# Cross attention: one product with V moved ahead inside its step, and one exponential ahead of an eviction

## What is computed

```
q_c = _ln(x) @ W_qc + b_qc
kv_c = _ln(context) @ W_kvc + b_kvc
k_c, v_c = jnp.split(kv_c, 2, axis=-1)
...
c_attn_w = jax.nn.softmax(jnp.einsum('bhqd,bhsd->bhqs', q_c, k_c) * scale, axis=-1)
c_attn_out = jnp.einsum('bhqs,bhsd->bhqd', c_attn_w, v_c)
```

## Time and profile before

| | us |
|---|---|
| median of 3 runs | 2712.4 |
| lowest, highest | 2710.79, 2716.66 |
| the profiled execution | 2714.79 |
| its span | 2712.8 |

### The profile page before, as it was taken

One profiled execution on the slowest core, in us unless ns is written; L12 is line 12 of the kernel. 1 busy time (PEld: TensorE's weight loads), 2 busy tenths in 40 slices (PEclk: granted clock), 3 DMA queues, 4 the chain that ended last, 5 costly groups with the idle time before them and its releaser, 6 DMA issues. The chain is left out here.

```text
span 2712.8 us, 49884 instructions
## 1 busy us (share of the span) xinstructions
PE 2616.2 (96%) x18548; PEld 2150.8 (79%) x18548; DVE 1708.4 (63%) x3413; ACT 1126.3 (42%) x2187; POOL 1303.5 (48%) x1447
## 2 busy tenths in 40 slices
PE   8899999999789999999999999999799999999997
PEld 6688888888578888888888888887478888888886
DVE  6677777776727777777777777776654444444431
ACT  4354444444434555555555555554432212212210
POOL 1445445454415777777777777767611221220211
PEclk9999999999889999999999999999799999999999
DMA  7454545545243444444444444334231111111110
GB/s 221 127 131 118 130 124 137 129 117 153 85 131 98 113 113 112 109 112 113 118 113 111 111 120 117 107 89 124 83 113 36 43 47 36 43 47 36 43 43 24
DMA packets 190609, 269.86 MB, mean 99 GB/s; under 512 B 32769, under 2 KB 110593, under 8 KB 190353
## 3 DMA queue, kind: packets, MB, share of 16 engines
q1 hardware_dynamic: 187296, 259.33, 35.4%
q0 software_dynamic: 3072, 7.34, 0.8%
HBM read 111.11 MB, written 36.77 MB: 55 GB/s over the span
## 5 line engine op out<-in xcount | busy, mean ns | idle before, releaser
L1639 ACT ACTIVATE cross_prT<-cross_tr_ps 125x448 f32<-125x448 f32 x768 | 407.4, 544 | 285.0 <-PE cross_tr_ps L1389 275.9
L1517 DVE TENSOR_REDUCE cross_parts<-cross_sc_ps 112x1 f32<-112x500 f32 x512 | 336.9, 664 | 213.3 <-PE cross_sc_ps L1375 212.0
L1690 POOL TENSOR_TENSOR cross_part<-cross_prT 125x448 f32<-125x448 f32 x252 | 291.7, 1157 | 212.8 <-PE cross_or_ps L1409 113.7
L1013 POOL TENSOR_TENSOR self_psum<-self_prT 112x224 f32<-112x224 f32 x256 | 180.9, 707 | 331.0 <-ACT self_prT L903 321.0
L1389 PE MATMUL cross_tr_ps<-cross_qst,cross_kst 98*125 98x224 f32 x1536 | 312.7, 287 | 3.8 <-ACT cross_prT L1639 3.3
L1389 PEld LDWEIGHTS cross_tr_ps<-cross_qst,cross_kst 98*125 98x125 f32 x1536 | 256.7, 189 | 62.0 <-ACT cross_prT L1639 23.3
L1692 POOL TENSOR_TENSOR cross_part<-cross_part,cross_prT 125x448 f32<-125x448 f32 x252 | 291.5, 1157 | 19.8
L2087 ACT ACTIVATE mlp_hv<-mlp_h_ps,mlp_b 128x512 f32<-128x512 f32 x112 | 76.9, 687 | 520.1 <-PE mlp_h_ps L73 506.1
L1375 PE MATMUL cross_sc_ps<-cross_kst,cross_qst 96*112 96x500 f32 (+1 forms) x1024 | 262.6, 337 | 3.2 <-DVE cross_parts L1517 3.0
L2004 DVE CAST mlp_hT_h<-mlp_hv 128x512 fp32r<-128x512 f32 x112 | 53.4, 477 | 320.0 <-ACT mlp_hv L2087 320.0
L903 ACT ACTIVATE self_prT<-self_st_ps 112x448 f32<-112x448 f32 x256 | 138.2, 541 | 187.3 <-PE self_st_ps L485 186.9
(11 more groups left out here) (274 smaller groups left out, 6742.2 us busy)
## 6 DMA issues: line engine op xcount, KB each, us to landing
cross_kst<-cross_nat_h SPq DMA_DIRECT2D x512, 93.8 KB, 2.2
cross_c_in<-in_context SPq DMA_DIRECT2D x96, 250.0 KB
cross_kst<-cross_nat_l SPq DMA_DIRECT2D x256, 93.8 KB, 2.2
cross_qst<-qc SPq DMA_DIRECT2D x192, 112.0 KB, 2.5
self_kst<-self_nat_h SPq DMA_DIRECT2D x128, 112.0 KB, 2.3
self_qst<-self_natq_h SPq DMA_DIRECT2D x128, 112.0 KB, 3.0
self_x_in<-in_x SPq DMA_DIRECT2D x16, 448.0 KB, 3.8
self_kst<-self_nat_l SPq DMA_DIRECT2D x64, 112.0 KB, 2.3
```

Of the source, the lines that this page charges most:

```text
L1013: pool.tensor_tensor(psum[:, j], prT[:, j, 0], prT[:, j, 1], ALU.add).then_inc(p_summed, 1)
L1517: dve.tensor_reduce(parts[:, g % 2, j, u, 0:1], sc_ps[u][0:QN, 0:SHALF[0]], AX_X, ALU.max, negate=True).then_inc(maxed, 1)
L1639: act.activation(prT[:, slot(h), 2 * c:2 * c + 2], bank(h, c)[0:SN, 0:2 * N].rearrange("p (k t) -> p k t", k=2), ACT.Exp).then_inc(exped, 1)
L1690: pool.tensor_tensor(part[:], prT[:, j, 0:2], prT[:, j, 2:4], ALU.add).then_inc(pre_summed, 1)
```

## The change

The number 2 is added to PV_EARLY.

```diff
--- before.py
+++ after.py
@@ -1136,7 +1136,7 @@
                 [("k", 3, 0)], [("v", 1)], [("k", 3, 1), ("c", 0), ("c", 1)], [("v", 2), ("c", 2)], [("v", 3)], [("v", 4), ("c", 3)],
                 [("c", 4)], [("v", 5), ("c", 5)]]
 
-        PV_EARLY, TILE_EARLY = (6, 14), (("c", 0), ("c", 4))
+        PV_EARLY, TILE_EARLY = (2, 6, 14), (("c", 0), ("c", 4))
         ORDER = [f for step in FILL for f in step]
 
         FIRST = [("k", g, half) for g in range(KC) for half in range(2)] + [("v", t) for t in range(ST)]
```

## The result

| | before | changed |
|---|---|---|
| median, us | 2713.7 (13 runs) | 2720.1 (13 runs) |
| lowest, highest | 2710.8, 2716.9 | 2717.2, 2722.0 |
| ratio to before | | 1.0023, 95% interval 1.0015 to 1.0032 |
| profiled execution and its span | 2714.8, 2712.8 | 2721.8, 2719.7 |

The changed kernel is 6.4 us slower, with an interval of 4.1 to 8.7. The prediction had 2717.8, 5.4 us over the median of 2712.4 known then, with 2713.5 to 2721.0 as its range.

The account below looks back on a forecast made before the run. TensorE, busy for 96% of the span, was taken as the bound. Bodies 1 to 14 lose 11 x 0.38 + 0.3 = 4.5 us, body 15 0.9: 5.4 over 2712.4 gives 2717.8 us, range 2713.5 to 2721 (8 in 10).

Parts of the forecast that it names:

- The wait for normalize: TensorE, step 2, main term: the early product would wait 0.46 us for VectorE's normalize, as in step 6.
- Behind the product: Step 2, TensorE going from product to projection: leaving costs 0 to 0.10 us, taken as 0.02; each body loses 0.38.
- Transfers of the row maxima: Step 2 in 3 of 14 bodies: earlier loss to the transfer vanishes beneath the new wait; these lose 0.3 us together.
- ScalarE's swap: ScalarE, step 1: third exponential ahead of the eviction, ending before normalize; the later eviction has 0.85 us of cover, no cost.
- VectorE's lateness: VectorE takes step 2's maxima after the product; split maxima end about 1465.1, 0.8 us of cover before step 4's projection.
- Bodies 15 and 16: Early product at 1.2 GHz in body 15 adds 0.9 us (0.7 to 1.2); body 16 nothing, beneath GpSimd.
- -1.2 at the full clock: Body 15: early product meets 2.4 GHz, takes 2.40 not 4.64, gains 1.2 us; total 2715.7; chance 0.07.
- The first (no wait): Step 2: normalize ready in time or TensorE regains the wait; 1.1 us gained, 2711.3; chance 0.12, including part of it.
- The third (VectorE late in step 3): Step 4's projection waits for split maxima; at 0.4 us a body, total 11, 2723; chance 0.12 with other additions.
- The fourth (the exponential decides): Step 2's product waits for the exponential, forecast to end 0.4 us before normalize; chance within the forecast's 0.65.
- no path to a gain of 5.4 us: Claim that gaining over 5.4 us needs more TensorE idle time in bodies 1 to 14 than 5.7 and 0.7.

## Why the prediction was right, and where not

**The wait for normalize: right.** The forecast had a new wait of 0.46, read from step 6's rows, and 0.77 from the turned scores to the product; 0.77 was measured. Three experiments hang the loss on it: hidden (0.9997); lengthened by 0.59 (14 x 0.59 = 8.3 forecast, 8.9 between the medians, 9.0 in the traces' bodies 1 to 14); taken away (28 waits of 0.46 would be 12.9; 12.4 between the medians, 10.2 in the traces, where a body that no transfer holds up is 0.84 shorter and the transfers hold up TensorE again).

**Behind the product: the term that was mis-sized.** I bounded the cost of leaving the product by 0 and 0.10 and took 0.02, since a projection's matmul is long enough to hide a weight load. The trace has 0.28 between its first two and not 0.18: 0.10, the upper end and what turned scores pay. From normalize to step 3's projection it is 6.44 (1466.34 - 1459.90), the upper end of the 6.34 to 6.44 that I had named. The stretch loses 0.46 and not 0.38, the whole period 0.41, and bodies 1 to 14 lose 5.3 us and not 4.5. The Trainium skill, TensorEngine Tiling (Array Packing), section Tiling Modes, says that a change of tiling mode drains TensorE; the prediction quoted it and kept it as an upper end. These rows agree with it in so far as the projection pays the same 0.10 as turned scores do; the 0.05 of the context tiles they do not explain. The step that failed was reading that 0.05 as a sign that the cost shrinks with the work behind it. The prediction also called the product the only work in 32-column tiles. The sums of the denominators (L1409) are in such tiles too, in the earlier trace rows: in body 9 after the change the turned scores behind their 8 matmuls take 1470.54 - 1470.23 = 0.31 to the projection and not 0.22, so they pay much the same.

**How close the number came is in part luck.** The median lies 2.3 us above the forecast, and 1.3 of that is the median of the kernel before, which went from 2712.4 with 3 runs to 2713.7 with 13. The increase of 6.4 has an interval of 4.1 to 8.7, which holds 5.4 and would hold 4.5 as well. In the profiled pair the bodies lost 0.8 more than forecast, body 15 and what hangs on it gained 1.05 where 0.9 more was forecast, and 2.8 us of the difference lie ahead of the bodies and behind them, where the change moves nothing and where kernels that are alike differ by some 3 us.

**Transfers of the row maxima: right in kind.** They lay beneath the new wait in body 5 and all but 0.16 in body 13. They occur in other bodies in another run, so the 0.3 us is a sample.

**ScalarE's swap and VectorE's lateness at no cost: right.** The swap alone gives 1.0002. VectorE's split maxima end 0.82 before the projection of step 4 in body 9 (1469.72 and 1470.54), and no wait for them appears in bodies 1 to 14.

**Bodies 15 and 16: not settled by the profile.** The forecast had +0.9 at the lower clock and named -1.2 at the full clock as a rival. The changed kernel's profiled execution met the full clock, and from step 14's product of body 14 to step 6's of body 16 it took 84.71 us against 85.76, 1.05 less, near the rival's 1.2. The added idle stretch of 1.50 us, which the prediction held against this rival, was not followed by the lower level in this execution. But the early product took 4.09 and 3.98 to the next start in two other kernels (the early product alone; in bodies 15 and 16 alone), and there the stretch took 85.57 and 85.94. The product at the end of the step ran at either level too, and four kernels that have it there differ by more than the terms in question: 84.1 to 85.8. The timed pair gives 0.9996, which holds both.

**The rivals.** The first (no wait) is out. The third (VectorE late in step 3) is out. The fourth (the exponential decides) is out: it ended 0.34 before normalize, 0.4 forecast, and with ScalarE's old order some 0.1 before it.

**A sentence that was wrong.** I saw no path to a gain of 5.4 us, since TensorE had only 5.7 and 0.7 us of waits to give; but these are 6.4, more than 5.4. The change itself touched none of them. The 5.7 are those that the list shows as idle; each wait is 0.46 long and not 0.41, and the reordering of VectorE took all 14, 6.2 us.

**What stays open.** Whether GpSimd alone sets the end of body 15 was not shown; the experiment was too small for the measurement. Why leaving the product costs 0.10 ahead of one kind of work and 0.05 ahead of another was not tried. In the experiment with step 6's product late, the shares of the product's place and of ScalarE's order were not told apart.

## What to carry to other kernels

Work on the bound engine may go early only as far as what it waits for is ready there; read that from the last wait at a sister place that is already early. What an early place is worth is what it covers: in a step with nothing between two dependent groups, having 2.4 us of matmuls between them (and the exponential ahead of the eviction) was worth more than a wait of 0.46; in a step with a projection there, it was worth nothing. Where the wait is on another engine's queue, look for what stands ahead in that queue without need: here moving two instructions of VectorE forward, at no added work, gained 6.2 us, where moving the work of TensorE that waits had lost 6.4.

## What the runs showed of the hardware that I had not expected

Leaving the 24 matmuls in 32-column tiles cost 0.10 us in front of a projection's matmul that streams 376 columns, as it does in front of turned scores that stream 224, where context tiles that stream 125 pay 0.05. TensorE started 0.15 us after the end of VectorE's normalize in every case looked at (1472.74 to 1472.89, 1460.28 to 1460.43, 1459.09 to 1459.24, 1538.32 to 1538.47). Once it started 0.06 after the end of ScalarE's exponential (1454.14 to 1454.20), so that way is no longer than 0.06. And in body 15 the same early product, behind the same idle 1.5 us, ran at 2.4 GHz in one kernel (2.41 us to the next start) and in part at 1.2 GHz in two others (3.98 and 4.09).
